# Two graph layers on one core: one product of 512 columns for both layers, and VectorE's word work moved ahead of the norm

## What is computed

```
a   = adj.astype(float)
x1  = layernorm(x + concat(a @ x / rowsum(a), x) @ weight + bias)
h   = x1 @ W.T                       e_j = h @ a[128:]
h2  = softmax_over_j(where(adj == 0, -inf, e_i + e_j)) @ h
out = layernorm(x1 + h2)
```

## Time and profile before

| | |
|---|---|
| median of 3 runs | 1012.83 us (1010.03 to 1012.96) |
| the profiled execution | 1011.9 us, its span 1010.2 us |
| mean granted PE clock | 0.989 |
| PE busy | 970.8 us, 96% |
| PEld busy | 866.9 us, 86% |
| DVE busy | 732.5 us, 73% |
| ACT busy | 601.8 us, 60% |
| POOL busy | 277.1 us, 27% |
| chain that ended last | PE 61%, DMA 27%, ACT 7%, issue 3%, DVE 2% |
| moved from and to HBM | 286.46 MB read, 13.76 MB written |

### The profile page before, as it was taken

The page is one execution under the profiler, slowest core; times in us unless marked ns, Lnnn a source line. Parts: engine busy times, 40 slices in busy tenths (PEclk is TensorE's granted clock), DMA queues, the critical chain, the costliest instruction groups (busy, mean ns, idle before and its releaser), DMA issues.

```text
span 1010.2 us, 22065 instructions
## 1 busy us (share of the span) xinstructions
PE 970.8 (96%) x8727; PEld 866.9 (86%) x8727; DVE 732.5 (73%) x1791; ACT 601.8 (60%) x604; POOL 277.1 (27%) x275
## 2 busy tenths in 40 slices
PE   6899889999999998999999999999999999999996
PEld 6899767888988897888898888888888888888885
DVE  3698887888877786778777676666654986677674
ACT  3988898888878887988868676767421000000000
POOL 4345544333435433434333333332000000000000
PEclk9999989999998999999999999999999999999999
DMA  9999999999999999999999999999421022222101
GB/s 283 394 420 420 421 420 421 419 421 421 421 421 417 420 418 422 415 419 414 410 392 362 420 344 349 341 350 311 159 77 71 22 84 86 90 90 89 34 24 34
DMA packets 50490, 301.70 MB, mean 299 GB/s; under 512 B 6608, under 2 KB 7888, under 8 KB 17360
## 3 DMA queue, kind: packets, MB, share of 16 engines
q0 software_dynamic: 37344, 270.03, 66.9%
q1 hardware_dynamic: 12336, 29.47, 8.7%
q10 hardware_dynamic: 704, 0.75, 0.3%
HBM read 286.46 MB, written 13.76 MB: 297 GB/s over the span
## 4 chain that ended last, share of the span: by engine, by line
PE 61%; DMA 27%; ACT 7%; issue 3%; DVE 2%; POOL 0%; ACTq 0%; DVEq 0%
PE ps_agg L403 33%; DMA adj_in<-in_adj_dram,chunk 26%; PE ps_part L403 22%; ACT edges L585 5%; PE ps_y L403 4%; PE ps_h L752 1%; ACT parts L576 1%; PE ps_h L707 0%; DMA x_all<-in_x_dram 0%; DVE parts L911 0%; PE ps_x1T L745 0%; POOL adj_in L1399 0%; DVE packed L963 0%; DVE edgesT L948 0%; PE ps_y L707 0%
## 5 line engine op out<-in xcount | busy, mean ns | idle before, releaser
L403 PE MATMUL ps_agg<-parts,edgesT 128*128 128x255 f16 (+1 forms) x5240 | 592.3, 274 | 20.3 <-DVE edgesT L948 18.9
L403 PEld LDWEIGHTS ps_agg<-parts,edgesT 128*128 128x128 fp8e4 x5240 | 514.2, 98 | 85.7 <-DVE edgesT L948 24.2
L585 ACT ACTIVATE edges<-adj_in 128x2048 fp8e4<-128x2048 int32 x256 | 481.2, 1905 | 62.8 <-DMA adj_in<-in_adj_dram,chunk 61.2
L1399 POOL DMA_INDIRECT adj_in<-in_adj_dram,chunk x256 | 272.2, 1063 | 430.4 <-ACT edges L585 419.7
L948 DVE STREAM_TRANSPOSE edgesT<-edges 128x512 uint32<-128x512 uint32 x256 | 167.1, 691 | 60.2 <-ACT edges L585 59.6
L403 PE MATMUL ps_part<-parts,edgesT 128*128 128x256 f16 x1664 | 190.2, 273 | 0.3 <-DVE parts L1050 0.3
L403 PEld LDWEIGHTS ps_part<-parts,edgesT 128*128 128x128 fp8e4 x1664 | 162.8, 98 | 18.8 <-DVE parts L1050 0.5
L652 ACT ACTIVATE std<-mean_var,eps 128x1 f32<-128x1 f32 x64 | 18.9, 295 | 226.4 <-DVE mean_var L1224 226.4
L963 DVE SCALAR_TENSOR_TENSOR packed<-edgesT,packed 128x2048 uint32<-128x2048 uint32 x48 | 109.6, 2283 | 1.2 <-DVE packed L959 0.5
L403 PE MATMUL ps_part<-parts,packed 128*128 128x256 f16 x772 | 87.2, 273 | 0.0
L403 PEld LDWEIGHTS ps_part<-parts,packed 128*128 128x128 fp8e4 x772 | 75.6, 98 | 8.7
(11 more groups left out here) (125 smaller groups left out, 655.3 us busy)
## 6 DMA issues: line engine op xcount, KB each, us to landing
adj_in<-in_adj_dram,chunk POOLq DMA_INDIRECT x256
adj_in<-partial_sums SPq DMA_DIRECT2D x16, 256.0 KB, 5.7
out_dram<-edges SPq DMA_DIRECT2D x60, 64.0 KB, 3.3
partial_sums<-partial SPq DMA_DIRECT2D x13, 256.0 KB
packed_adj<-parts SPq DMA_DIRECT2D x2, 1024.0 KB
adj_in<-packed_adj SPq DMA_DIRECT2D x2, 832.0 KB, 5.1
x_all<-in_x_dram POOLq DMA_DIRECT2D x6, 256.0 KB, 13.1
x_all<-in_x_dram SPq DMA_DIRECT2D x6, 256.0 KB, 14.8
```

Source lines behind the costliest of these rows:

```text
L403: done = eng.matmul(bank[:, 0:cols], rows[:, n // BYTES, n % BYTES, :], moving[:, n, :], start=(n == first), stop=(n == last))
L585: act.activation(edges[:, r // 2, r % 2, :], adj_in[:, m % SLOTS, :], ACT.Copy, scale=EDGE[t % GROUP], saturate=False).then_inc(s_conv, 1)
L1399: pool.indirect_dma_start(adj_in[:, m % SLOTS, :], None, adj_chunks, bass.IndirectOffsetOnAxis(chunk[:, 0:1], 0), element_offset=first_row ...
```

## The change

- Before, layer one and layer two took one product each for a block that both need. Now the rows of both layers lie side by side (`both`, 512 columns) and one product serves both. A product of 512 columns fills a whole bank, so layer two's part of the sum lies in `ps_agg` (two banks in turn) and `ps_part` is no longer used for it.
- PE's order in an inline tile: first block 0 with 512 columns, then the blocks that only layer one needs with 255 columns, then `hidden(t-3)`, then the wait for `s_lo1` and blocks 1 to 4(g-1)-1 with 512 columns. `s_agg`, on which DVE's residual waits, is raised after the last of these.
- DVE's order in step t from 13 on: pack, check, join and catch (`words_of`) stand right behind the transposes of t, ahead of residual and moments of t-1.
- Catching goes in five rounds at tiles 12 to 23 instead of three: bands 0 and 1 of groups 0 and 1 (two tiles of words in a step), three bands of group 2 (one in a step), then bands 2 and 3 of groups 0 and 1 (two in a step), into two banks in turn. Groups 0, 1 and 2 have 4, 4 and 3 bands caught, before 2, 3 and 4.
- Two more partial sums are stored and loaded back, and added on DVE.
- SP stores the kept words one group later, and POOL clears one more column of `parts0`.

The core of the diff:

```diff
+    ROUNDS = [(0, 0, 2, 12, 2), (1, 0, 2, 14, 2), (2, 0, 3, 16, 1), (0, 2, 2, 20, 2), (1, 2, 2, 22, 2)]
...
-            def first_layer(t):
+            def bank_ready(t):
                 pe.wait_ge(s_tr, NQ * (t + 1))
                 wait(pe, s_z, t - 1)
+                if inline(t - 2):
+                    pe.wait_ge(s_partk, t - 2 - EARLY + 1)
...
+            def first_layer(t):
+                words, done = by_bands(edgesT[:, t % 2, :]), GROUP * bands_of(t // GROUP)
+                bank_ready(t)
...
+                else:
+                    contract(pe, ps_agg[t % 2], words, both, [0], 0, done - 1)
+                    contract(pe, ps_agg[t % 2], words, parts0[:, :, 0:LO + KEPT_F], range(done, NBLK), 0, done - 1)
+
+            def both_layers(t):
+                done = GROUP * bands_of(t // GROUP)
+                pe.wait_ge(s_lo1, bands_of(t // GROUP))
+                contract(pe, ps_agg[t % 2], by_bands(edgesT[:, t % 2, :]), both, range(1, done), 0, done - 1)\
+                    .then_inc(s_agg, 1)
...
             def step(t):
                 if on(t, 0) and t > 0:
                     for r in range(NQ):
                         transpose(t, r)
+                if inline(t - 1):
+                    words_of(t)
...
                 if inline(t - 1):
                     keep_partial(t - 1)
-                joins = GROUP <= t < 2 * GROUP * PAIRS + GROUP and t % (2 * GROUP) == 0
...
+                if not inline(t - 1):
+                    words_of(t)
...
                 for n in KEEP_UNTIL:
-                    if g == KEEP_UNTIL[n] - 1:
+                    if g == KEEP_UNTIL[n]:
                         store_words(n)
...
+                for i, k in enumerate(SECOND):
+                    if c == 0 and g == ROUNDS[k][0]:
+                        dve.wait_ge(s_partld2[i], 16)
+                        dve.tensor_tensor(part_in[:, s, :], part_in[:, s, :], part_in[:, 5 + i, :], ALU.add)\
+                            .then_inc(s_pjoin, 1)
...
+            pool.memset(parts0[:, :, LO + KEPT_F:2 * F], 0.0)
```

More of the change, by code:

```diff
@@ L49, in bass_two_graph_layers @@
     GCOLS = F + 1
[L50 removed]
+    BOTH = 4 * F
+    SECOND_HI, SECOND_LO = 2 * F, 3 * F
     LO = F
@@ L328, in bass_two_graph_layers @@
         s_partld = [sem(f"partial_landed{s}") for s in range(5)]
+        s_partld2 = [sem(f"partial_of_second_round_landed{g}") for g in range(len(SECOND))]
+        s_pjoin = sem("rounds_added")
         s_unp = sem("unpacked")
@@ L752, in hidden, with caught @@
                 pe.matmul(ps_h[:, 0:HCOLS], x1T[:, :], w1_cols[:, :], start=True, stop=True).then_inc(s_h, 1)
-            def second_layer_inline(t):
-                bands = bands_of(t // GROUP)
-                if t == EARLY:
-                    pe.wait_ge(s_vkept, GROUPS)
-                pe.wait_ge(s_lo1, bands)
-                wait(pe, s_partk, t - EARLY)
-                contract(pe, ps_part, edgesT[:, t % 2, :], weighted_rows, range(0, bands * GROUP), 0, bands * GROUP - 1)\
-                    .then_inc(s_part, 1)
-            def caught(i):
-                blocks = GROUP * CAUGHT[i // GROUP]
+            def caught(i, k):
+                g, first, bands, at, by = ROUNDS[k]
+                blocks = range(GROUP * bands)
                 if i == 0:
@@ L785, in _ @@
                 if inline(t):
-                    second_layer_inline(t)
-                if catching(t):
-                    caught(t - CATCH)
+                    both_layers(t)
+                for i, k, c in caught_at(t):
+                    caught(i, k)
                 if t == 7:
@@ L1073, in _, with words_of @@
             odd_groups = range(1, 2 * PAIRS, 2)
+            def words_of(t):
+                joins = GROUP <= t < 2 * GROUP * PAIRS + GROUP and t % (2 * GROUP) == 0
+                if on(t, 0) and not joins:
+                    if t % (2 * GROUP) == 1 and t > 1:
+                        pack(t - 1)
+                    pack(t)
+                if t // GROUP in odd_groups and t % GROUP == GROUP - 1:
+                    check(t // GROUP, 0)
+                if on(t, 1) and (t - 1) % GROUP == GROUP - 1 and (t - 1) // GROUP not in odd_groups:
+                    check((t - 1) // GROUP, 0)
+                if on(t, 2) and (t - 2) % GROUP == GROUP - 1 and (t - 2) // GROUP not in odd_groups:
+                    check((t - 2) // GROUP, 1)
+                if joins:
+                    check(t // GROUP - 1, 1)
+                    join(t // (2 * GROUP) - 1)
+                for i, k, c in caught_at(t):
+                    unpack_caught(i, k, c)
+                for i, k, c in caught_at(t - 1):
+                    keep_caught(i, k)
             def step(t):
```

143 lines of the change are left out of this document (69 added, 74 removed).

## The result

The changed kernel takes 1059.98 us (median of 4 runs, 1055.32 to 1067.96) against 1011.43 us for the kernel before, measured beside it: ratio 1.0478, 95% interval 1.0443 to 1.0514. That is 48.6 us more, where +14 was forecast. The direction was right; the size was more than three times too small, and the time lies far outside the range of 1014 to 1036. The profiled execution of after took 1067.96 us, the longest of the four; its span is 1065.8 us, 55.6 more than before. The two long executions of after (1067.96 and 1064.12) had a mean granted clock of 0.970, the two short ones (1055.32 and 1055.85) 0.978 and 0.981.

The account below looks back on a forecast made before the run. Loads were taken to set the pace up to tile 35, PE from there. Terms 11.2 + 7.5 - 3.2 - 3.5 + 0.7 + 1.6 = +14.3 gave 1026.2, forecast 1027 us, range 1014 to 1036.

Parts of the forecast that it names:

- Step 1: PE, tiles 36 to 63: each pair of products becomes one of 512 columns at 215.8 ns, saving 3.2 us.
- the rival at 975 us: PE, tiles 36 to 63: a 512-column product takes the skill page's 131 ns; about 975 us, chance 0.01.
- the one with no saving at all: PE: a 512-column product costs as much as two old ones; +3.2, 1030 us, inside the forecast's range.
- Step 2: ACT and DVE, tiles 13 to 31: words ahead of the norm close a new loop; +11.2 us at tile 36.
- the ring: Loop of conversions, transposes, words, moments and deviation on ACT, PE and DVE: 10.35 us a tile, plus 16 us of catching.
- Step 3: PE in every fourth tile waits for the newest weighted band with less cover; +7.5 us, bounds 5 to 12.
- other edits: Remaining edits: later stored words move 1 MB (2.4 us) of DMA past tile 35, costing nothing while the ring rules.
- Step 4: Phase of turns: 32 products leave it, -3.5 us; two additions of partial sums and lighter turns, +0.7 us.
- Step 5: Between tile 63 and the turns: its moments and weighting now delay the last x1 transposition; +1.6 us.
- The hidden ring: Rival, up to tile 35: loads still come last and only the waits remain; +1.8, 1015 us, chance 0.09.
- Faster: Rival, PE from tile 36: saved and moved products decide; 1002 or 1005 us, chance 0.08.
- The low clock: Rival, PE after waits at every fourth tile and idle time at tiles 16 and 24: up to 3 us each; 1036, 0.13.

Follow-up runs that it names:

- alone512: Changed kernel with words behind the norm, s_lo1 wait only before last four blocks, three old catching rounds, reductions a step later, kept words stored as before: 1010.91 us.
- ring_only: Changed kernel with split s_lo1 wait, second place for caught sums, reductions a step later, kept words stored earlier; words still ahead of the norm: 1020.00 us.
- two_parts: Changed kernel with a second buffer for the caught partial sums of odd rounds: 1049.38 us, ratio 1.0362.
- all_mended: ring_only with pack, check, join and catch put back behind the norm, nothing else changed: 1011.06 us, ratio 0.9993 to the kernel before.
- extremes_moved: Changed kernel with the four input-check reductions (L1105) moved from steps 40, 44, 48, 52 to 41, 45, 49, 53: 1048.32 us.
- before_words_first: Kernel before with one edit: from step 13 pack, check, join and catch stand ahead of residual and moments: 1018.67 us, ratio 1.0065.
- all_mended_last: all_mended with the two layers of tile 63 multiplied apart again, in two banks: 1006.41 us, ratio 0.9945 to the kernel before.
- alone512_last: alone512 with the two layers of tile 63 multiplied apart again: 1011.42 us, ratio 0.9988 to the kernel before.
- order_back: Changed kernel with pack, check, join and catch put back behind residual, moments and partial sum: 1066.61 us, ratio 1.0537.
- whole_pieces: Changed kernel with the caught sums' single buffer in its own place, 2 KB in one piece per partition: 1047.07 us, ratio 1.0371.
- store_early: Changed kernel with the kept words of the first two pairs stored one group earlier, as before: 1054.94 us, ratio 1.0433.

## Why the prediction was right in sign and far off in size

**Step 1, products of 512 columns: right.** The rows of a stream at full clock, start and length:

```profile
412.47 5.83 PE ps_agg L415 x27
```

5.83 / 27 = 215.9 ns, forecast 215.8. The rows of tiles 41 and 60 without a loss say the same: 55 products took 12.04 us and 35 took 7.72, so 20 more took 4.32, 216.0 ns each. So the rival at 975 us is dead, and so is the one with no saving at all (218.4 ns). The Trainium skill, "TensorE: Matmul & The Clock Gate", section Back-to-back issue gap, has two values for 512 columns: N/2.4 + 2.5 gives 215.8 ns, and the row agrees; 131 ns for a stream with weight loads is contradicted by it. From tile 36 to 64 alone512 takes 2.3 and ring_only 3.2 us less than before, forecast 3.2.

**Step 2, the ring: right in mechanism, near in size, wrong in what it took for free.** +11.2 us at tile 36 were forecast; two_parts shows 9.2, ring_only 8.3, and the medians of ring_only and all_mended differ by 9. That is above the lower bound of 5.5. What failed is the silent part, a term put at nothing: of the catching it priced unpacks, copies and sums on DVE and the DMA's bytes, but not that `keep_caught` overwrites a buffer that a store has to have read. The change has four changes of round where two were, its stores go in 512-byte pieces, and with the words ahead of the norm the whole wait is paid; DVE waits 15.7 us (two_parts: 16.0 less in the profiles, 10.6 in the medians). That the trace before had no such wait was no evidence that it stays so. This term alone is larger than the ring. Tile 32 was forecast for 379 us and began at 395.

**Step 3, the wait for `s_lo1`: right table, mis-sized term.** 7.5 us forecast, 28.7 measured (17.8 idle, 10.9 low clock). The table of waits came out to 0.2 us once the reductions were moved (extremes_moved). Missing were, first, the reductions L1105 at steps 40, 44, 48 and 52: 2.2 us each, 6.5 us of PE's waits in tiles 44 to 52, while in tile 40 the cause named next hides it. They stood in the code and in the trace of before, in the steps that the table goes through; I had costed that way from step 16, where they don't occur. Second, the store of the kept words, 6.4 us of ACT in step 40, which "other edits" priced by its bytes, at 2.4 us, and judged harmless; in the new layout it took 46.3 us, in the old one 9.6 (before_words_first). Third, the low clock. The bound of 12 was too low for all three; "the upper end is for the clock" left 4.5 us for what was 10.9.

**Step 4, caught blocks: right.** -3.5 and +0.7 us forecast for the turns, -3.3 in all_mended_last against before and -3.8 against alone512_last, which has the same seam and the old rounds; the +0.7 for the two additions of partial sums doesn't show.

**Step 5, from tiles to turns: right for the way that it counted, with the clock left out.** +1.6 forecast, up to the last x1 transposition; there alone512 and all_mended show +1.9. The turns as a whole are 4.0 longer in alone512, where nothing else moves that stage: most of the rest, 1.7 us, comes where the granted clock was 0.66 behind PE's wait of 2.35 us. In all_mended the same wait brought no low clock, and splitting tile 63 gave back 2.5. In after, 4.0 and the -3.5 of step 4 about cancel: +0.2.

**The rivals.** The hidden ring (1015) falls by before_words_first: the ring costs 6.6 us in the kernel before, without any of the other edits. "Faster" needs `weighted_lo` within 1.4 us, and the waits of 1.7 to 4.9 us say no. The low clock was given 0.13 with up to 3 us each: it did cost up to 2.9 us each, but as one of several surprises. No rival had the stores. That the sign was right is owed to the ring and the wait, both there as forecast; the size was missed by terms that the sum did not have. The chances stood on the terms that I had, and the range on their bounds; a term left out has no bound. order_back shows the same failing in an expectation: it priced what the edit frees and not what it puts in the way.

**Not tried.** The changed kernel with its kept words in longer pieces. The 9.6 us of the old layout say that the wait of step 40 would go, but no run shows what that is worth.

## What to carry to other kernels

Where a wait comes near the path, list every instruction that stands ahead of its signal in each single step that it occurs in, not in one typical step, and look for those that come only every fourth time. Where a buffer is refilled, compare the distance between its last write and the next first one with the time that its reader takes, from issue to landing and with the queues as full as they are in that stage; and see what is queued behind the writer. Where a layout is changed, look at everything that is stored from the same room: the bytes stay, but the pieces may become shorter. A joint product delays the earliest of its results to the end of the last one: keep it apart where the next stage begins on that result, as in the last tile here.

## What the runs showed of the hardware that was not expected

Beside loads that fill the DMA engines a store takes longer in short pieces. 1 MB took 9.6 us in pieces of 8 KB and 43.9 in pieces of 512 bytes, at 422 and 421 GB/s of all DMA. 256 KB of caught sums took 7.5, 9.6, 12.8 (before_words_first) and 11.2 us (whole_pieces) in pieces of 2 KB, and 14.2, 14.6, 19.4 (alone512) and 14.6 to 15.4 us (after) in pieces of 512 bytes; single ones of these lie lower in other kernels, down to 8.9 us in two_parts.

What TensorE's clock costs after a short wait is not fixed by the length of the wait. Both rows of tile 60 follow 2.15 us of idle time, and 55 products took 13.73 us in after and 12.04 in extremes_moved. Their windows of 5 us (after, then extremes_moved), then that of tile 40 in store_early, after 2.85 us:

```profile
751.00:756.00 5.00, 4.27 (x12) 1.61 (x13) 3.15 (x8) 4.99 (x6) 0.94 (x1) 0.66 0.95 382
```

```profile
735.00:740.00 5.00, 4.41 (x21) 2.04 (x22) 3.18 (x7) 4.99 (x6) 0.94 (x1) 1.00 0.96 367
```

```profile
482.00:487.00 5.00, 4.42 (x21) 2.06 (x22) 4.86 (x9) 5.00 (x5) 2.76 (x3) 1.00 1.00 416
```

PEclk 0.66 in the first, that is 1.2 GHz for part of it, and 1.00 in the two others, although the last follows a longer wait. At the seam, too, waits of 2.35 us led to a granted clock of 0.66 in alone512 and 1.00 in all_mended. Over the six waits of after, 1.7 to 4.9 us long, the loss was 0 to 2.9 us. What decides it, these runs don't say.
